# A decoder of two layers on one core: context loaded transposed, row vectors in two transfers, new priorities

## The chip, the cores and the metric

The kernel runs on one core of one Trainium2 chip. The metric is the device time of one execution in microseconds (us), lower is better. The core has five engines that matter here: PE (TensorE, matrix products; its weight loads are listed apart as PEld), DVE (VectorE), ACT (ScalarE), POOL (GpSimd), and SP (SyncE), which only issues transfers (DMA). Each engine works off its own queue in order, and semaphores order the engines among each other.

## The reference

Sixteen entries of 256 tokens with 256 features pass through two decoder layers in float32. Each of six sub-blocks is followed by a residual sum and a layer norm (`LN`, without weights):

```
x = LN(x + attn0(x))          # layer norm, q, k, v; ELU+1 feature maps; a 16 x 16 mix over the heads of each token;
                              # output product; then an MLP of width 1024 with GELU
x = LN(x + xattn0(x, ctx))    # 16 heads, keys and values from the context, window of 64 tokens to each side
x = LN(x + ffn0(x))           # six attention nodes of 8 heads, each fed by earlier nodes
x = LN(x + attn1(x))          # linear attention, causal cumulative sum
x = LN(x + xattn1(x, ctx))    # 16 heads, normed q and k, keys from the context, padding mask
x = LN(x + ffn1(x))           # product in the Fourier domain, plus a bias
```

`ctx` (16 x 256 x 256) enters twice: as keys and values of `xattn0`, and as keys and values of `xattn1`.

## The kernel before

Two partition blocks of 128 tokens (or features) and 256 columns make one slot of 128 x 512 float32; an entry has ten slots (`slot(s, n)`), and four entries are in flight (`NS = 4`, s = entry mod 4). An entry is loaded when the entry four before it is finished. A product needs its input with the features on the partitions. So nearly every product is preceded by a transposition on PE: `transposes` (line 704, matmuls against an identity at line 707) makes four 128 x 128 transposes into a PSUM bank, and an engine copies them out. For the context there are two such steps in each entry: `ctx_t` at the start (from slot RAW into slot CT, copied by ACT at line 1393) for the products `x_k` and `x_v` of the first cross attention, and `ctx_t2` late (a second load, named `again`, into slot AGAIN, and again copied into CT) for `y_k` and `y_v` of the second. CT is also the home of node 0 of the feed-forward in between, which is why the context is brought a second time.

`tokens` (line 711) and `features` (line 719) are the two forms of a 256 x 256 x 256 product: eight matmuls at lines 714 and 722. Attention scores are computed at lines 872 and 897, their maxima at 1233 (DVE), exponentials at 1466 (ACT), and the products with the values at 925. The mix of the first attention block runs on POOL (lines 1614 and 1624) with sums on DVE (1199, 1203).

The order of the work is not written out by hand. `entry_steps()` lists the 510 steps of an entry, each with its engine, an assumed duration, and the steps that it needs; `setup_steps()` does the same for the set-up, which folds weight matrices into each other. `program_plan()` then plays all 16 entries and the set-up through, and at each free engine takes the ready step of the earliest entry with the largest `tail`, the longest chain of durations that hangs on it. Each tail is multiplied with a random factor:

```
    rng = np.random.default_rng(720053)
    lean = [0.0 * v for v in rng.random(len(steps))]
    tail = [t * (1 + 0.3 * v) for t, v in zip(tail, rng.random(len(steps)))]
```

The result, `PLAN`, is the fixed queue of every engine. Weights of most products are streamed through a ring of four slots by SP, between the other transfers. The row vectors (13 biases and norm vectors, 256 long, copied to all partitions, tile `row`) come in one transfer of 1664 KB, which SP issues behind the operands of set-up node 2. They are needed first by DVE at line 1189, which adds the biases to q, k and v.

Of the kernel before, what the change touches and what calls it, by code (L numbers as in the profile page):

```python
# [11 lines left out]
ACT = mybir.ActivationFunctionType  # L12
AX = mybir.AxisListType.X

P = 128
# [53 lines left out]
ROWS = ["a_qb", "a_kb", "a_vb", "a_ob", "proj_b", "x_bo", "ln_g", "ln_b", "y_bq", "y_bk", "y_bo", "f_b", "n5_b"]  # L69
RSLOT = {n: i for i, n in enumerate(ROWS)}  # L70

SLOTS = 10
X, CT, XT = 0, 1, 2
RAW, AGAIN, Z = 6, 7, 7
# [20 lines left out]
SINGLE = range(4, BANKS)  # L95

# [49 lines left out]
def entry_steps():  # L146
# [13 lines left out]
    def layer_norm(n, ready, *also):  # L160
# [6 lines left out]
    ctx_t = through("ctx_t", 0, 0.44, "ACT", 0.49, load)  # L167
    z = layer_norm(1, load)
    z_t = through("z_t", 0, 0.44, "ACT", 0.9, z)
    raw = [through("a_qkv", a, 1.75, "DVE", 0.61, z_t, ("PE", "ctx_t", 0),  # L170
                   *((("PE", "a_qkv", a - 1),) if a else ()), also=(ctx_t,))
# [29 lines left out]
    x_k = through("x_k", 0, 1.75, "ACT", 1.8, ctx_t, ("PE", "z2_t", 0))  # L201
# [46 lines left out]
    for c in range(NODES):  # L248
# [11 lines left out]
        if c == NODES - 1:  # L260
            again = do("SP", "again", 0, 2.6, cv[c])
            ctx_t2 = through("ctx_t2", 0, 0.44, "ACT", 0.48, again, ck[c])
            y_k = through("y_k", 0, 1.75, "DVE", 0.66, ctx_t2, ("DVE", "centre", "y_k"))
            y_k = do("ACT", "y_k", 0, 0.48, y_k)
            y_k = do("DVE", "y_ks", 0, 0.6, y_k)
            y_k = do("ACT", "y_ks", 0, 0.5, y_k)
            y_k = do("DVE", "y_kn", 0, 0.65, y_k)
# [51 lines left out]
def program_plan():  # L319
# [14 lines left out]
    rng = np.random.default_rng(720053)  # L334
    lean = [0.0 * v for v in rng.random(len(steps))]
    tail = [t * (1 + 0.3 * v) for t, v in zip(tail, rng.random(len(steps)))]
# [59 lines left out]
    while events:  # L396
# [10 lines left out]
        for e in waiting:  # L407
            blocked = set()
            for i, t, n in sorted(waiting[e], key=lambda w: (
                    ((2.5 if e == "SP" else 1.5) if w[0] < 0 else w[0]) + (0 if kept_mode(w[2]) else 0.5) + lean[w[2]], w[1], w[2])):  # L410
# [64 lines left out]
def build(nc, x, ctx_in, mask, w_all, w_setup, cols, rows, ew, act_w, out):  # L475
    ctx = ExitStack()
    with ctx:
# [53 lines left out]
        in_vec = signal("s_loaded_vectors", 16)  # L531
        in_rows = signal("s_loaded_rows", 16)
# [11 lines left out]
        signals = ([setup_pe, setup_vec, setup_act, setup_pool, in_vec, in_rows, in_fourier] + list(in_w.values()) + in_ring + in_node + evicted  # L544
# [120 lines left out]
        def tensor(e):  # L665
# [76 lines left out]
            for i, op, a, units in PLAN["PE"]:  # L742
# [52 lines left out]
                elif op == "ctx_t":  # L795
                    e.wait_ge(*when("ctx", i))
                    transposes(take("misc", "ctx_t", i), slot(s, RAW)).then_inc(*tell(pe[s], "ctx_t mm", i))
                elif op == "ctx_t2":
                    e.wait_ge(*when("ctx again", i))
# [994 lines left out]
```

## Time and profile before

| | |
|---|---|
| median of three runs | 3605.32 us (3601.53 to 3610.42) |
| span of the profiled execution, first to last instruction | 3599.7 us |
| median less span (what lies around it) | 5.6 us |
| mean granted clock of PE over the span | 0.974 of full speed |
| busy: PE, DVE, ACT, POOL | 3245.1, 2282.5, 1713.9, 1019.3 us |
| transfers | 122.88 MB, mean 34 GB/s |

The profile comes from one further execution, whose own time is known as its span. Busy time of matmuls is modelled, since they overlap: the duration of one is longer than the distance to the next.

### The profile page before, as it was taken

The page shows a single profiled execution, that of the slowest core. Times are in us where ns is not written, and L with a number is a line of the kernel's source. Part 1 is how long each engine was busy: PE and PEld are TensorE (multiplying, and loading weights), DVE is VectorE, ACT ScalarE, POOL GpSimd, SP SyncE. Part 2 cuts the span into 40 slices and gives each one's busy share as a digit, 9 for nine tenths or more (in the row PEclk, how much of TensorE's full clock was granted, in tenths as well). Part 3 has the DMA queues.
Part 4 walks back from the last instruction along what each step waited for, and adds up shares of the span by engine and source line. Part 5 has one row for each costly group of instructions (what it writes and reads, how often), then busy time and mean ns, then how long its engine had stood idle before and what let it go on. Part 6 is the DMA issues. An engine that isn't in the chain of part 4 may idle for free.

```text
span 3599.7 us, 77605 instructions
## 1 busy us (share of the span) xinstructions
PE 3245.1 (90%) x31500; PEld 2402.1 (67%) x31500; DVE 2282.5 (63%) x4093; ACT 1713.9 (48%) x3466; POOL 1019.3 (28%) x795
## 2 busy tenths in 40 slices
PE   7899989999989989999999999999999999998876
PEld 6777666666676667766666776666677666766654
DVE  6665757647766766667676666767667576465633
ACT  1245454544545454554545555454555545554532
POOL 7942305103242504214060421506042150000000
PEclk9899999999999999999999999999999999999987
DMA  6211010100011101011010101101010110000000
GB/s 213 71 45 39 22 42 16 31 31 22 23 51 31 36 13 49 25 35 35 17 45 16 48 25 31 36 19 45 16 48 25 31 35 15 31 16 13 13 7 4
DMA packets 123132, 122.88 MB, mean 34 GB/s; under 512 B 9760, under 2 KB 122656, under 8 KB 122656
## 3 DMA queue, kind: packets, MB, share of 16 engines
q1 hardware_dynamic: 122784, 117.91, 10.9%
q8 instruction: 258, 4.23, 0.5%
q14 instruction: 90, 0.74, 0.1%
HBM read 113.69 MB, written 4.19 MB: 33 GB/s over the span
## 4 chain that ended last, share of the span: by engine, by line
PE 61%; DVE 13%; POOL 9%; ACT 8%; issue 7%; DMA 1%; SPq 0%; DVEq 0%; POOLq 0%; ACTq 0%
PE banks L722 16%; PE banks L714 13%; PE banks L897 7%; PE banks L925 6%; PE banks L872 6%; DVE nmx L1233 5%; POOL work L1614 5%; ACT work L1466 4%; POOL work L1624 3%; PE banks L707 2%; PE banks L883 2%; PE banks L729 2%; PE banks L932 2%; PE banks L901 1%; PE banks L1004 1%
## 5 line engine op out<-in xcount | busy, mean ns | idle before, releaser
L722 PE MATMUL banks<-work,weights 128*128 128x256 f32 x3584 | 861.9, 388 | 40.5 <-DVE work L1256 22.1
L1233 DVE TENSOR_REDUCE nmx<-banks 128x4 f32<-128x1024 f32 (+1 forms) x640 | 720.9, 1165 | 251.5 <-PE banks L872 249.1
L722 PEld LDWEIGHTS banks<-work,weights 128*128 128x128 f32 x3584 | 671.3, 192 | 177.1 <-issue 55.2
L1466 ACT ACTIVATE work<-banks 128x1024 f32<-128x1024 f32 (+1 forms) x640 | 596.5, 980 | 268.7 <-PE banks L901 266.9
L714 PE MATMUL banks<-weights,work 128*128 128x256 f32 x2688 | 661.0, 392 | 44.0 <-ACT work L1466 16.6
L714 PEld LDWEIGHTS banks<-weights,work 128*128 128x128 f32 x2688 | 505.0, 195 | 147.3 <-issue 47.7
L1624 POOL TENSOR_TENSOR work<-work 128x512 f32<-128x512 f32 x256 | 405.5, 1609 | 212.3 <-DVE work L1203 115.7
L897 PE MATMUL banks<-work 32*128 32x256 f32 (+1 forms) x5120 | 396.2, 396 | 46.2 <-issue 15.6
L872 PE MATMUL banks<-work 32*128 32x256 f32 (+1 forms) x5120 | 355.0, 393 | 36.2 <-issue 11.0
L1250 DVE TENSOR_TENSOR added<-work 128x1024 f32<-128x1024 f32 x192 | 261.5, 1363 | 171.7 <-ACT work L1466 164.1
L925 PE MATMUL banks<-work 128*32 128x256 f32 (+3 forms) x5632 | 334.6, 359 | 23.7 <-ACT work L1466 23.6
L1614 POOL TENSOR_TENSOR work<-work 128x512 f32<-128x512 f32 x256 | 341.0, 1358 | 49.8 <-DVE work L1199 32.2
L1658 POOL TENSOR_TENSOR work<-work,row 128x512 f32<-128x512 f32 x64 | 88.8, 1387 | 882.1 <-PE banks L707 882.1
L897 PEld LDWEIGHTS banks<-work 32*128 32x128 f32 x5120 | 213.3, 189 | 165.8 <-issue 97.3
L872 PEld LDWEIGHTS banks<-work 32*128 32x128 f32 x5120 | 234.9, 187 | 128.9 <-issue 108.3
L1365 ACT ACTIVATE work<-banks,cb 128x256 f32<-128x256 f32 x384 | 161.4, 473 | 251.7 <-PE banks L722 251.6
L925 PEld LDWEIGHTS banks<-work 128*32 128x32 f32 x5632 | 156.6, 110 | 163.8 <-issue 102.4
L1203 DVE TENSOR_REDUCE work<-work 128x32 f32<-128x512 f32 x256 | 173.1, 679 | 90.8 <-POOL work L1624 90.6
L1199 DVE TENSOR_REDUCE work<-work 128x32 f32<-128x512 f32 x256 | 172.2, 680 | 75.2 <-POOL work L1614 75.0
L1450 ACT ACTIVATE work<-banks 128x256 f32<-128x256 f32 x320 | 118.7, 385 | 189.7 <-PE banks L883 189.1
L707 PE MATMUL banks<-ident,work 128*128 128x128 f32 x896 | 140.1, 286 | 68.8 <-DVE work L1181 28.3
L901 PE MATMUL banks<-work,ones_bf 3*128 3x256 bf16 (+1 forms) x2560 | 191.4, 272 | 0.0
(157 smaller groups left out, 3518.3 us busy)
## 6 DMA issues: line engine op xcount, KB each, us to landing
weights<-in_w_all SPq DMA_DIRECT2D x322, 256.0 KB, 2.7
work<-in_w_setup SPq DMA_DIRECT2D x41, 256.0 KB, 5.5
work<-in_ctx SPq DMA_DIRECT2D x32, 256.0 KB, 2.9
work<-in_x SPq DMA_DIRECT2D x16, 256.0 KB, 3.0
out<-work SPq DMA_DIRECT2D x16, 256.0 KB, 2.2
weights<-in_w_all SPq DMA_DIRECT2D x1, 3072.0 KB, 16.9
row<-in_rows SPq DMA_DIRECT2D x1, 1664.0 KB, 10.1
mrow<-in_mask SPq DMA_DIRECT2D x16, 32.0 KB, 3.1
```

The costliest lines, as they stand in the source:

```text
L707: ins = e.transpose(b[:, f * 256 + c * P:f * 256 + c * P + P], src[:, c, f * P:f * P + P], ident[:, :])
L714: ins = e.matmul(b[:, m * 256:m * 256 + 256], xin[:, k, m * P:m * P + P], wslot(w)[:, k, :], start=(k == 0 and (m == 0 or closed)) if star ...
L722: ins = e.matmul(b[:, m * 256:m * 256 + 256], wslot(w)[:, k, m * P:m * P + P], xin[:, k, :], start=(k == 0 and (m == 0 or closed)) if star ...
L872: ins = e.matmul(b[g // 2][:, g % 2, cc * 256:cc * 256 + kk.stop - kk.start], q[32 * g:32 * g + 32, f, cc * P:cc * P + P], k[32 * g:32 * g ...
L897: e.matmul(b[g // 2][:, g % 2, o], k[32 * g:32 * g + 32, f, kc * P:kc * P + P], q[32 * g:32 * g + 32, f, qq], start=(kind != "x"), stop=False,
L901: ins = e.matmul(b[g // 2][:, g % 2, o], ones_bf[32 * g:32 * g + 3, :], upper(stored_nmax(s, a))[32 * g:32 * g + 3, qq], start=False, stop ...
L925: ins = e.matmul(b[32 * g:32 * g + 32, lo:hi], left, right[:, kc * 256 + lo - qq.start:kc * 256 + hi - qq.start], start=(kc == 0), stop=(k ...
L1233: e.tensor_reduce(nmax(s, n)[:, 2 * p:2 * p + 2, :], b, AX, ALU.max, negate=True).then_inc(*freed("max", n, p, i))
L1250: e.tensor_tensor(added[:, half], pt(half, 0, 4)[:, :, 0:S], pt(half, 0, 4)[:, :, S:2 * S], ALU.add).then_inc(*tell(vec[s], "added", a, i))
L1466: e.activation(dst, src, ACT.Exp).then_inc(*freed("exp", n, p, i))
L1614: e.tensor_tensor(big1, q.unsqueeze(2).broadcast_to([P, PH, NH, DH]), k.unsqueeze(1).broadcast_to([P, PH, NH, DH]), ALU.mult).then_inc(*te ...
L1624: e.tensor_tensor(big2, mix.unsqueeze(2).broadcast_to([P, PH, DH, NH]), v.unsqueeze(1).broadcast_to([P, PH, DH, NH]), ALU.mult).then_inc(* ...
```

## The change

1. The host hands `ctx` over with tokens and features exchanged. Each load goes straight into CT, and the steps `ctx_t` and `ctx_t2`, their PE transposes and their ACT copies are gone. The products `x_k`, `x_v` and `y_k` wait for the transfer itself. The second load may be issued once `ck` of node 5 has read CT; before, it waited for `cv` of node 5. The bytes and the form of the transfer stay the same.
2. The row vectors come in two transfers: the first three rows (biases of q, k and v) behind the first entry's `x`, the other ten behind the second entry's `x`; the one transfer behind node 2's operands is gone.
3. The tails are multiplied by five random factors in a row, one of up to 1.3 and four of up to 1.08, from other seeds. With the steps that are gone, this gives every engine another order.

```diff
@@ -164,11 +166,10 @@
     kept = do("DVE", "kept", 0, 0.9, load)
-    ctx_t = through("ctx_t", 0, 0.44, "ACT", 0.49, load)
     z = layer_norm(1, load)
     z_t = through("z_t", 0, 0.44, "ACT", 0.9, z)
-    raw = [through("a_qkv", a, 1.75, "DVE", 0.61, z_t, ("PE", "ctx_t", 0),
-                   *((("PE", "a_qkv", a - 1),) if a else ()), also=(ctx_t,))
+    raw = [through("a_qkv", a, 1.75, "DVE", 0.61, z_t,
+                   *((("PE", "a_qkv", a - 1),) if a else ()))
            for a in range(3)]
@@ -198,7 +199,7 @@
     x_t = through("x_t", 0, 0.44, "ACT", 0.48, x)
-    x_k = through("x_k", 0, 1.75, "ACT", 1.8, ctx_t, ("PE", "z2_t", 0))
+    x_k = through("x_k", 0, 1.75, "ACT", 1.8, ("PE", "z2_t", 0))
     x_v = through("x_v", 0, 1.75, "ACT", 0.56, clear)
@@ -258,10 +259,9 @@
         if c == NODES - 1:
-            again = do("SP", "again", 0, 2.6, cv[c])
-            ctx_t2 = through("ctx_t2", 0, 0.44, "ACT", 0.48, again, ck[c])
-            y_k = through("y_k", 0, 1.75, "DVE", 0.66, ctx_t2, ("DVE", "centre", "y_k"))
-            y_k = do("ACT", "y_k", 0, 0.48, y_k)
+            again = do("SP", "again", 0, 2.6, ("PE", "ck", c))
+            y_k = through("y_k", 0, 1.75, "DVE", 0.66, again, ("DVE", "centre", "y_k"), also=(("PE", "co", c - 1),))
+            y_k = do("ACT", "y_k", 0, 0.48, y_k, ("PE", "cv", c))
             y_k = do("DVE", "y_ks", 0, 0.6, y_k)
@@ -331,9 +331,9 @@
 
-    rng = np.random.default_rng(720053)
-    lean = [0.0 * v for v in rng.random(len(steps))]
-    tail = [t * (1 + 0.3 * v) for t, v in zip(tail, rng.random(len(steps)))]
+    for n, seed in enumerate(SEEDS):
+        spread = 0.08 if n else 0.3
+        tail = [t * (1 + spread * v) for t, v in zip(tail, np.random.default_rng(seed).random(len(steps)))]
     first, last = place["SP", "load", 0], place["DVE", "ln_n", 9]
@@ -407,7 +407,7 @@
             for i, t, n in sorted(waiting[e], key=lambda w: (
-                    ((2.5 if e == "SP" else 1.5) if w[0] < 0 else w[0]) + (0 if kept_mode(w[2]) else 0.5) + lean[w[2]], w[1], w[2])):
+                    ((2.5 if e == "SP" else 1.5) if w[0] < 0 else w[0]) + (0 if kept_mode(w[2]) else 0.5), w[1], w[2])):
                 if not idle[e]:
@@ -792,12 +793,6 @@
                     product(take("misc", "four", a), FOURIER[a][1]).then_inc(*tell(setup_pe, "four mm", a))
-                elif op == "ctx_t":
-                    e.wait_ge(*when("ctx", i))
-                    transposes(take("misc", "ctx_t", i), slot(s, RAW)).then_inc(*tell(pe[s], "ctx_t mm", i))
-                elif op == "ctx_t2":
-                    e.wait_ge(*when("ctx again", i))
-                    transposes(take("misc", "ctx_t2", i), slot(s, AGAIN)).then_inc(*tell(pe[s], "ctx_t2 mm", i))
                 elif op == "z_t":
@@ -837,11 +832,12 @@
                 elif op == "x_k":
-                    e.wait_ge(*when("ctx_t", i))
+                    e.wait_ge(*when("ctx", i))
                     arrived("x_k")
...
                     e.wait_ge(*when("cleared", i))
+                    e.wait_ge(*when("ctx", i))
                     arrived("x_v")
@@ -1028,7 +1024,7 @@
                 elif op == "y_k":
-                    e.wait_ge(*when("ctx_t2", i))
+                    e.wait_ge(*when("ctx again", i))
                     once("centred", "y_k", NH)
@@ -1183,9 +1179,7 @@
                     e.wait_ge(*when("a_qkv mm", a, i))
-                    once("rows")
-                    if a == 0:
-                        e.wait_ge(*when("ctx_t mm", i))
+                    once("first rows")
                     e.tensor_tensor(slot(s, A_QKV[a]), halves(at("a_qkv", a, i)), r_(("a_qb", "a_kb", "a_vb")[a]),
@@ -1385,12 +1379,9 @@
                         *freed("four", a))
-                elif op in ("ctx_t", "ctx_t2", "o_t", "x_t", "r_t", "y_t", "f_t"):
-                    dst = CT if op[:3] == "ctx" else XT
+                elif op in ("o_t", "x_t", "r_t", "y_t", "f_t"):
                     e.wait_ge(*when(f"{op} mm", i))
-                    if op == "ctx_t2":
-                        e.wait_ge(*when("ck mm", 5, i))
-                    e.activation(flat(s, dst), at(op, i)[:, :], ACT.Copy).then_inc(*freed(op, i))
+                    e.activation(flat(s, XT), at(op, i)[:, :], ACT.Copy).then_inc(*freed(op, i))
                 elif op == "c_t":
@@ -1702,9 +1693,6 @@
                         operand(f"{n}{a}", in_node[a], "node operands", a)
-                    if a == 2:
-                        e.dma_start(row[:, :, :].rearrange("p r n -> p (r n)"), rows.partition_broadcast(P)).then_inc(
-                            *tell(in_rows, "rows"))
                 elif op == "fourier":
@@ -1719,12 +1707,18 @@
                     e.dma_start(slot(s, X), of_entry(x, i)).then_inc(*tell(in_x[s], "x", i))
-                    e.dma_start(slot(s, RAW), of_entry(ctx_in, i)).then_inc(*tell(in_ctx[s], "ctx", i))
+                    if i == 0:
+                        e.dma_start(row[:, 0:FIRST_ROWS, :].rearrange("p r n -> p (r n)"),
+                                    rows[0:FIRST_ROWS * D].partition_broadcast(P)).then_inc(*tell(in_first_rows, "first rows"))
+                    elif i == 1:
+                        e.dma_start(row[:, FIRST_ROWS:, :].rearrange("p r n -> p (r n)"),
+                                    rows[FIRST_ROWS * D:].partition_broadcast(P)).then_inc(*tell(in_rows, "rows"))
+                    e.dma_start(slot(s, CT), of_entry(ctx_in, i)).then_inc(*tell(in_ctx[s], "ctx", i))
                     e.dma_start(small[s]["mrow8"][:, :], mask[i:i + 1, :].broadcast_to([P, S])).then_inc(
...
                 elif op == "again":
-                    e.wait_ge(*when("cv mm", 5, i))
-                    e.dma_start(slot(s, AGAIN), of_entry(ctx_in, i)).then_inc(*tell(in_ctx[s], "ctx again", i))
+                    e.wait_ge(*when("ck mm", 5, i))
+                    e.dma_start(slot(s, CT), of_entry(ctx_in, i)).then_inc(*tell(in_ctx[s], "ctx again", i))
                 elif op == "store":
@@ -1776,7 +1770,7 @@
     arrays = {
-        "x": a["x"], "ctx": a["ctx_1024"], "mask": a["mask_BxS2_bk0"],
+        "x": a["x"], "ctx": a["ctx_1024"].transpose(0, 2, 1), "mask": a["mask_BxS2_bk0"],
         "w_all": np.concatenate([w[n] for n in W_LOADED]), "w_setup": np.stack([w[n] for n in W_SETUP]),
```

Left out are the constants (`FIRST_ROWS = 3`, `SEEDS = (66172, 467317, 360552, 577980, 753377)`, slots RAW and AGAIN gone), the new semaphore for the first rows, and one wait of the `y_k` squares on ACT, which is now on `cv` of node 5 instead of the transposes.

## Rows read from the trace of the kernel before

**Rows 1.** The page: span, busy table, and two lines of its 40 slices.

```profile
span 3599.7 us, 77605 instructions
...
PE 3245.1 (90%) x31500; PEld 2402.1 (67%) x31500; DVE 2282.5 (63%) x4093; ACT 1713.9 (48%) x3466; POOL 1019.3 (28%) x795
...
PE   7899989999989989999999999999999999998876
...
PEclk9899999999999999999999999999999999999987
```

**Rows 2.** Windows: us, then busy us of PE, PEld, DVE, ACT, POOL; clock, DMA share, GB/s.

```profile
518.50:728.00 209.50, 190.00 (x1938) 136.69 (x1937) 142.58 (x248) 104.75 (x209) 59.94 (x44) 0.96 0.08 24
728.00:946.70 218.70, 198.07 (x1979) 143.51 (x1978) 140.48 (x247) 103.71 (x210) 57.91 (x45) 0.98 0.08 23
946.70:1145.80 199.10, 182.42 (x1781) 136.16 (x1783) 136.10 (x249) 100.10 (x205) 63.68 (x49) 0.97 0.12 36
1145.80:1363.50 217.70, 198.44 (x1985) 145.21 (x1978) 141.77 (x255) 107.50 (x220) 61.83 (x47) 1.00 0.10 30
...
1574.60:1785.40 210.80, 195.18 (x1946) 144.18 (x1945) 140.52 (x253) 106.39 (x216) 63.84 (x47) 0.99 0.11 31
3469.50:3599.70 130.20, 83.53 (x720) 58.29 (x712) 51.45 (x100) 41.48 (x85) 4.51 (x6) 0.79 0.02 5
```

**Rows 3.** Waits of PE's matmuls, window 1574.6 to 1785.4: releaser, total, times, longest.

```profile
PE banks L722 <- DVE work L1256: 2.0, 1, 2.0
PE banks L925 <- ACT work L1466: 1.7, 2, 1.2
```

**Rows 4.** Groups by line: busy, mean ns of one, idle before.

```profile
L707 PE MATMUL banks<-ident,work 128*128 128x128 f32 x896 | 140.1, 286 | 68.8 <-DVE work L1181 28.3 <-DVE ykb L1089 10.2 <-ACT work L1466 7.4
...
L1393 ACT ACTIVATE work<-banks 128x512 f32<-128x512 f32 x112 | 66.1, 597 | 80.8 <-PE banks L707 80.6
```

**Rows 5.** Timeline near 1865: start, us, engine, line.

```profile
1864.88 0.37 SPq L1727 DMA_DIRECT2D work<-in_ctx  x1
...
1867.80 1.09 PE L707 MATMUL banks<-ident,work 128*128 128x128 f32 x8
...
1868.73 3.62 PE L714 MATMUL banks<-weights,work 128*128 128x256 f32 x16
```

**Rows 6.** Timeline near 373: start, us, engine, line.

```profile
373.25 0.63 PE L707 MATMUL banks<-ident,work 128*128 128x128 f32 x4
...
374.65 1.97 PE L714 MATMUL banks<-weights,work 128*128 128x256 f32 x8 [0.78 <-ACT work L1393]
```

**Rows 7.** Who waited for the copies of line 1393 (us, times).

```profile
  PEld banks L714: 6.6, 8
  PE banks L714: 4.4, 6
```

**Rows 8.** Timeline of the first 26 us.

```profile
11.40 1.28 ACT L1393 ACT_TABLE_LOAD   x1 [11.40 <-PE banks L707]
...
13.31 1.28 ACT L1349 ACT_TABLE_LOAD   x1
...
18.18 3.78 PE L714 MATMUL banks<-weights,work 128*128 128x256 f32 x8 [1.11 <-ACT work L1365]
...
23.84 0.69 DVE L1189 TENSOR_TENSOR work<-banks,row 128x512 f32<-128x512 f32 x1 [4.52 <-issue]
...
25.38 1.49 POOL L1605 TENSOR_SCALAR work<-work 128x512 f32<-128x512 f32 x1 [17.90 <-ACT work L1416]
```

**Rows 9.** Windows of the start, to 135.7.

```profile
0.00:78.00 78.00, 54.79 (x263) 47.18 (x264) 47.77 (x107) 13.85 (x25) 51.07 (x63) 0.93 0.77 246
78.00:135.70 57.70, 52.48 (x244) 45.04 (x243) 34.42 (x59) 12.67 (x24) 56.69 (x43) 0.91 0.23 74
```

**Rows 10.** Transfers of the start: the page's row of in_rows, and below.

```profile
row<-in_rows SPq DMA_DIRECT2D x1, 1664.0 KB, 10.1
```

**Rows 11.** Timeline near 40.8: PE behind a transfer of set-up weights.

```profile
40.76 5.28 PE L757 MATMUL banks<-col,work 128*128 128x1 f32 x24 [3.83 <-DMA work<-in_w_setup]
```

More of the change, by code:

```diff
@@ L69 @@
 ROWS = ["a_qb", "a_kb", "a_vb", "a_ob", "proj_b", "x_bo", "ln_g", "ln_b", "y_bq", "y_bk", "y_bo", "f_b", "n5_b"]
+FIRST_ROWS = 3
 RSLOT = {n: i for i, n in enumerate(ROWS)}
@@ L73 @@
 X, CT, XT = 0, 1, 2
-RAW, AGAIN, Z = 6, 7, 7
+Z = 7
 A_QKV, ELU, MIX, BIG1, BIG2 = (3, 4, 5), (6, 7), 6, (7, 8), (9, 2)
@@ L95 @@
 SINGLE = range(4, BANKS)
+SEEDS = (66172, 467317, 360552, 577980, 753377)
 def quad(n):
@@ L531, in build @@
         in_vec = signal("s_loaded_vectors", 16)
+        in_first_rows = signal("s_loaded_first_rows", 16)
         in_rows = signal("s_loaded_rows", 16)
@@ L543, in build @@
         stored = [signal(f"s_stored{s}", 16) for s in range(NS)]
-        signals = ([setup_pe, setup_vec, setup_act, setup_pool, in_vec, in_rows, in_fourier] + list(in_w.values()) + in_ring + in_node + evicted
+        signals = ([setup_pe, setup_vec, setup_act, setup_pool, in_vec, in_first_rows, in_rows, in_fourier] + list(in_w.values()) + in_ring + in_node + evicted
                    + pe + vec + act + pool + in_x + in_ctx + in_mask + stored)
@@ L1530, in scalar @@
                     e.wait_ge(*when(f"{op} raw", i))
-                    e.wait_ge(*(when("ctx_t2 mm", i) if op == "y_k" else when("y_k_t mm", i)))
+                    e.wait_ge(*(when("cv mm", 5, i) if op == "y_k" else when("y_k_t mm", i)))
                     e.activation(flat(s, Y_K_SQ if op == "y_k" else Y_Q_SQ), flat(s, Y_K if op == "y_k" else Y_Q), ACT.Square).then_inc(
```

## The prediction

> **What bounds the kernel now.** I read the page first. PE is busy 3245.1 of 3599.7 us; the next engine, DVE, has 2282.5 [rows 1]. The slices show PE at nine tenths or more from the second slice almost to the end, with a granted clock of full speed (2.4 GHz) nearly all the way; the exceptions are the first slices and the last two, 0.8 and 0.7 [rows 1]. So the middle is PE's, but not by its work alone. I then cut the trace at the SP issues that load the next entry, which come once per entry [rows 2]. The reader should see that the kernel falls into a cycle: the four windows from 518.5 differ (209.5, 218.7, 199.1, 217.7 us), and the seven windows between loads from 1363.5 to 2838.6 all take 210.1 to 211.2 us, one of which is shown. In that one PE works 195.18 of 210.8 us and idles 15.6. In the four before, idle is 19.5, 20.6, 16.7 and 19.3 us, 19.0 on average. From 518.5 to the last load at 2838.6 lie 11 such windows, and PE is as full for about two more, so one microsecond per cycle is 13 us of the result. Last I read the waits inside the cycle: the largest is 2.0 us on a DVE norm, the next 1.7 us on exponentials [rows 3]; the idle time is many short waits in a fixed order, and the longest are not on a context transposition. The start is another regime: POOL is busy 56.69 of the 57.7 us from 78 to 135.7, and 51.07 of the first 78 [rows 9]; it only starts its attention work at 25.38 [rows 8]. The last 130.2 us have PE at work for 83.5 [rows 2].
>
> **Transposes that go.** Each entry loses `ctx_t` and `ctx_t2`, four 128x128 transposes each: 2 x 4 x 16 = 128 of the 896 matmuls of line 707 [rows 4]. In the steady cycle `ctx_t2` stands beside another group of four: eight begin at 1867.80 and the next product at 1868.73, so eight cost 0.93 us of PE's queue [rows 5]. That is the lower bound: 16 x 0.93 = 14.9 us. The upper bound is their share of busy time, 128/896 x 140.1 = 20.0 us [rows 4]. I take 17. The page "TensorE: Matmul & The Clock Gate" of the Trainium skill, Part 4, gives some 275 ns for such a transpose in a kernel's context and says that the mode does not count as PE being busy. The trace shows a duration near that (286 ns mean, [rows 4]) but a spacing of 116 ns, since they overlap [rows 5]. By the page's figure as a cost, 128 x 0.275 = 35 us would go instead of 17.
>
> **Copies that go.** 32 copies of 597 ns on ACT, 19.1 us [rows 4]. ACT is busy 106.4 of 210.8 us in a cycle [rows 2], so the copies lie beside other work except where PE stood behind one. All 112 copies of that kind held PE's products up for 6.6 us of weight loads and 4.4 of matmuls [rows 7], which are largely the same stops; one of `ctx_t2` shows it with 0.78 us [rows 6]. The share of 32 in 112 of 4.4 to 6.6 is 1.3 to 1.9 us. I take 1.5, bounds 0 and 6.6. What is late next at these places is the matmul's other inputs: after the change `y_k` stands directly behind the second context transfer. In the cycle that was issued at 1864.88 and the transposes started 2.92 us later [rows 5]. The SP issue now waits for `ck` of the last cell instead of `cv`, earlier by at most one product of 1.97 us [rows 6]. So I cost this wait at nothing; if its cover were gone, it would be at most 2.9 us per entry, 46 us. The streamed weights queue behind that SP wait and are released no later than before. The stronger waits in the new code (`x_v` on "ctx", `y_k` squares on `cv` of cell 5 instead of the transposes) name things that are finished tens of microseconds before or are read by earlier PE work; nothing.
>
> **Rows in two parts, and the start.** The first DVE addition ran at 23.84, after 4.52 us of idle time which the profile puts to no engine [rows 8]: the row vectors, whose transfer takes 10.1 us [rows 10], so issued at about 23.84 - 10.1 = 13.7. The products before it began at 18.18 and take 3.78, so the rows cost 23.84 - 21.97 = 1.9 us. Three of the 13 rows are 3/13 of 1664 KB, 384 KB, and are now issued right behind the first `x`; they will be there. Further, ACT loads a table for the context copy at 11.40, copies, and loads the exponential table at 13.31 for the first layer norm [rows 8]. Without the copy the second load can take the place of the first: 1.9 us more. So POOL may begin up to 3.8 us sooner, and POOL is what bounds to 135.7. Against it: the other 1280 KB now go before the node operands of the set-up, 5.2 us at the 246 GB/s of that window [rows 9], and PE already stands 3.83 us behind such operands at 40.76 [rows 11]. Before, the rows went behind the first six of these but ahead of the others, so only the first node's products are later. Bounds: 3.8 us gained, 5.2 lost. I take 1.5 gained. The DMA share later in the kernel is a tenth [rows 2] and covers everything else; the bytes and the shape of the context transfer are the same.
>
> **Priorities.** This is the part that no row prices directly. Every queue of every engine comes out of the planner, and the new factors together with the steps taken out give another order. What can change is idle time, 15.6 us per cycle, and the ends. The rows bound it thus: an order whose cycles idle like the four first ones, 19.0 us, loses 13 x 3.4 = 44 us; one that halves the idle time gains 13 x 7.8 = 101 us, which no window here shows. The waits are short and many, so an order can shave some of them, and there are two steps fewer in each entry that have to find a free PSUM bank. I lean a little to the gaining side: 0.6 us per cycle, 8 us. That is a choice; the range keeps both ends in part.
>
> **Sum.** 17 + 1.5 + 1.5 + 8 = 28 us. The profiled execution spans 3599.7 us; the median of the three runs is 3605.32, 5.6 us more for what lies around the span. Both fall alike: span about 3572, time 3605.3 - 28 = 3577 us. Without the order's 8 us it is 3585.
>
> **Rivals.** (A) *The new cycle idles more.* The transposes are gone, but the order locks into cycles with the 19.0 us of idle time of the first four windows. Then 44 us are lost and 20 gained: 3629 us, slower. It needs more than 1.5 us of extra idle time per cycle to eat the gain, and (20 + 10.8)/13 = 2.4 us to be measurably slower. For it: nearly all early windows are like that [rows 2], and the present cycle is among the least idle ones seen. Against it: its waits are spread, so nothing in particular must grow. (B) *The PE time freed turns into waiting.* If a chain of DVE maximum, ACT exponential and PE sets the cycle, removing work that filled a gap gives nothing: only the start and some of the transposes remain, 5 us, 3600 us, no change. For it: after PE's products the waits that end last are on DVE and ACT [rows 3]. Against it: in [rows 5] eight transposes lie in an unbroken run of PE work. (C) *A distinctly better order.* Idle time falls by 3 us per cycle to 12.6: 39 us in place of 8, so 3605 - 20 - 39 = 3546 us. (D) *Transposes cost their full duration.* Each is worth its 286 ns, not its spacing, 128 x 0.286 = 37 us in place of 17: 3557 us. [rows 5] speaks plainly against it. That is what the clock gate page's figure above would give.
>
> **How the numbers follow.** No change from a change can be told within about 0.3%, 10.8 us: 3594.5 to 3616.1. Chances: my forecast 0.42, its own range 3560 to 3594; (C) 0.24, 3520 to 3560; (D) 0.03; (B) 0.18; (A) 0.13, 3616 to 3640. That makes faster 0.69, same 0.18, slower 0.13. The range 3532 to 3612 leaves out the far end of (C), most of (A), together less than 2 in 10.
>
> **What the profile after would show.** 768 transposes on PE instead of 896, each cycle with 8 fewer PE matmuls, and PE's busy time per cycle down from 195.2 to about 194; if it falls by 2 us or more, (D) is right. The first DVE addition at about 20 instead of 23.84, and POOL's first work at 21 to 22. Windows between loads, once they repeat, of 209 us: 210.8 less 0.93, 0.1 and 0.6. Idle time per cycle near 15; 19 means (A), 16.5 (B), 12.6 (C). At `y_k`, no PE wait on the context transfer. I would be wrong if the cycle differs by more than 2 us either way, or if the end, where 46.7 of 130.2 us are idle [rows 2], grows or shrinks by more than 10: either is the order's doing and could outweigh all that I could price.

## The result, and the profile after

The changed kernel takes 3643.05 us (median of four runs, 3636.48 to 3646.29), the kernel before in the same comparison 3603.64. The ratio is 1.0114, 95% interval 1.0099 to 1.0129: 41 us slower. I had forecast 28 us faster, 3577 us, with 3532 to 3612 as the range. Of what I had listed, rival (A) comes nearest (3629 us, its own range 3616 to 3640, chance 0.13), and the time lies beyond that range too.

The page of the kernel after, its busy table and the granted clock in 40 slices (compare [rows 1]):

```profile
span 3641.2 us, 77305 instructions
...
PE 3257.8 (89%) x31372; PEld 2389.2 (66%) x31372; DVE 2277.5 (63%) x4093; ACT 1697.2 (47%) x3433; POOL 992.9 (27%) x795
...
PEclk9999999998999999999999999999999999999987
```

PE's busy time has risen by 12.7 us although it has 128 matmuls fewer, and its idle time (span less busy) has risen from 354.6 to 383.4 us. The slices hardly show it (both rows have one slice of eight tenths in the first third), but the mean granted clock has gone from 0.974 to 0.967.

Windows from load to load, columns as in [rows 2]:

```profile
511.60:726.40 214.80, 194.17 (x1988) 139.55 (x1981) 138.77 (x251) 103.41 (x209) 59.89 (x44) 0.95 0.08 22
...
1580.50:1794.40 213.90, 196.53 (x1938) 143.77 (x1937) 141.26 (x252) 105.45 (x215) 60.60 (x47) 0.98 0.10 31
1794.40:2009.40 215.00, 197.01 (x1938) 143.79 (x1937) 141.32 (x252) 105.61 (x215) 60.66 (x47) 0.98 0.10 31
...
2224.50:2440.60 216.10, 198.94 (x1938) 144.87 (x1937) 141.40 (x252) 105.72 (x215) 60.64 (x47) 0.97 0.10 31
...
3511.00:3641.20 130.20, 81.94 (x728) 56.85 (x720) 51.35 (x100) 41.84 (x84) 4.50 (x6) 0.79 0.02 5
```

The kernel again falls into a cycle, but of 213.9 to 216.1 us: 215.2 on average over the seven windows from 1364.4 to 2870.6, in place of 210.7. The count of PE matmuls is 1938, eight fewer, as it should be. Still PE's busy time is 196.5 to 199 us in place of 194.9 to 196.3 in the seven windows of before, at a mean granted clock of 0.97 to 0.98 in place of 0.98 to 0.99, and idle time is 17.2 to 18.3 us in place of 14.8 to 15.6. The end (130.2 us, PE busy 81.9) is as before. PE's longest waits in one of these cycles (releaser, total us, times, longest):

```profile
PE banks L928 <- DVE added L1244: 2.6, 2, 1.6
PE banks L723 <- ACT work L1387: 2.4, 1, 2.4
PE banks L868 <- DVE nmx L1227: 2.2, 2, 1.6
```

The second of them, 2.4 us, is the one that matters in e9 below. It is a product that stands behind a copy by ACT (`c_t`), not behind anything that the context touches.

The start, in the timeline (start, us, engine, line):

```profile
11.25 1.28 ACT L1343 ACT_TABLE_LOAD   x1 [11.25 <-DVE mv L1158]
...
16.28 3.75 PE L715 MATMUL banks<-weights,work 128*128 128x256 f32 x8 [1.20 <-ACT work L1359]
...
20.52 0.66 DVE L1183 TENSOR_TENSOR work<-banks,row 128x512 f32<-128x512 f32 x1
...
22.77 2.95 POOL L1596 TENSOR_SCALAR work<-work 128x512 f32<-128x512 f32 x2 [15.31 <-ACT work L1407]
```

There is one table load on ACT's way to the first layer norm, the first product starts at 16.28 instead of 18.18, the first DVE addition at 20.52 instead of 23.84, and POOL at 22.77 instead of 25.38 [rows 8]. The two transfers of the rows, size and us to landing:

```profile
row<-in_rows SPq DMA_DIRECT2D x1, 1280.0 KB, 9.5
...
row<-in_rows SPq DMA_DIRECT2D x1, 384.0 KB, 4.6
```

The instructions that move the context, their landing time, and who waited for them:

```profile
L1716 SPq DMA_DIRECT2D work<-in_ctx x16: 433/497/681, 3.6 to 2871.1; - x16
L1721 SPq DMA_DIRECT2D work<-in_ctx x16: 367/368/368, 354.1 to 3515.3; - x16
...
who waited for it (us, times):
busy tenths in 40 slices 0000000000000000000000000000000000000000
DMA to landing us min/median/max: 2.6/2.9/9.3
```

Nobody is listed: no engine waited for a context transfer, first or second.

### The profile page after: what moved, and what is told of

Same layout as the page of the kernel before. It is cut to its first block, busy times and chain, and to the rows that moved or that the text cites. A ratio compares the mean times of both kernels' runs of the same rounds, so it can differ in the third digit from the quotient of the medians.

```text
span 3641.2 us, 77305 instructions
## 1 busy us (share of the span) xinstructions
PE 3257.8 (89%) x31372; PEld 2389.2 (66%) x31372; DVE 2277.5 (63%) x4093; ACT 1697.2 (47%) x3433; POOL 992.9 (27%) x795
## 4 chain that ended last, share of the span: by engine, by line
PE 58%; DVE 20%; issue 8%; ACT 7%; POOL 6%; DMA 1%; SPq 0%; DVEq 0%; POOLq 0%; ACTq 0%
PE banks L723 17%; PE banks L715 12%; DVE nmx L1227 7%; PE banks L893 6%; PE banks L868 6%; PE banks L921 5%; POOL work L1615 3%; PE banks L831 3%; ACT work L1457 2%; POOL work L1605 2%; PE banks L730 2%; PE banks L928 2%; DVE work L1193 2%; DVE added L1244 1%; PE banks L879 1%
## 5 line engine op out<-in xcount | busy, mean ns | idle before, releaser
L723 PEld LDWEIGHTS banks<-work,weights 128*128 128x128 f32 x3584 | 678.8, 194 | 182.8 <-issue 50.1
L1615 POOL TENSOR_TENSOR work<-work 128x512 f32<-128x512 f32 x256 | 401.9, 1578 | 205.3 <-DVE work L1197 117.6
L893 PE MATMUL banks<-work 32*128 32x256 f32 (+1 forms) x5120 | 410.1, 407 | 46.5 <-DVE nmx L1227 17.9
L868 PE MATMUL banks<-work 32*128 32x256 f32 (+1 forms) x5120 | 365.4, 403 | 49.4 <-DVE nmx L1227 31.2
L1605 POOL TENSOR_TENSOR work<-work 128x512 f32<-128x512 f32 x256 | 327.5, 1293 | 77.1 <-DVE work L1193 61.0
L868 PEld LDWEIGHTS banks<-work 32*128 32x128 f32 x5120 | 243.6, 193 | 137.4 <-issue 114.2
L893 PEld LDWEIGHTS banks<-work 32*128 32x128 f32 x5120 | 216.5, 194 | 174.1 <-issue 78.4
L1250 DVE TENSOR_TENSOR work<-banks,work 128x256 f32<-128x256 f32 x192 | 80.3, 419 | 251.8 <-ACT work L1471 251.7
L879 PE MATMUL banks<-ident,nmx 128*128 128x128 f32 x640 | 131.5, 296 | 72.0 <-DVE nmx L1235 37.6
```

The source lines that it names most:

```text
L723: ins = e.matmul(b[:, m * 256:m * 256 + 256], wslot(w)[:, k, m * P:m * P + P], xin[:, k, :], start=(k == 0 and (m == 0 or closed)) if star ...
L868: ins = e.matmul(b[g // 2][:, g % 2, cc * 256:cc * 256 + kk.stop - kk.start], q[32 * g:32 * g + 32, f, cc * P:cc * P + P], k[32 * g:32 * g ...
L893: e.matmul(b[g // 2][:, g % 2, o], k[32 * g:32 * g + 32, f, kc * P:kc * P + P], q[32 * g:32 * g + 32, f, qq], start=(kind != "x"), stop=False,
L1605: e.tensor_tensor(big1, q.unsqueeze(2).broadcast_to([P, PH, NH, DH]), k.unsqueeze(1).broadcast_to([P, PH, NH, DH]), ALU.mult).then_inc(*te ...
L1615: e.tensor_tensor(big2, mix.unsqueeze(2).broadcast_to([P, PH, DH, NH]), v.unsqueeze(1).broadcast_to([P, PH, DH, NH]), ALU.mult).then_inc(* ...
```

## The experiments

For each kernel I also give the "planned end": the time at which `program_plan()` finishes its own play of the queues on its assumed durations. It is a number that the kernel's own planner computes, not a time of the chip; it is 3489 for before and 3507 for after.

**e1: the order kept.** The code of the kernel after, but the queues come from the steps and factors of the kernel before, with the context steps struck out. Shown is the line that strikes them; the rest of the edit puts the old steps and factors back into the planner.

```diff
+    plan = {e: [step for step in q if step[1] not in ("ctx_t", "ctx_t2")] for e, q in plan.items()}
     return plan, ring
```

> The code of the kernel after (context straight into CT, rows in two parts), but every engine's queue in the order of the kernel before, with only the ctx_t and ctx_t2 steps struck out. Theory 'order' (the loss comes from the new priorities, and the steps taken out are worth what I priced): 3604 - 20 = about 3585 us, range 3575 to 3592, cycle between loads about 209.6 us. Theory 'removal' (PE waiting for the second context transfer, or gaps left where the transposes stood, lose the time): 3625 us or more, cycle above 212. Theory 'freed time turns into waiting' (rival B): 3598 to 3604.

Measured: 3591.94 us, ratio 0.9974 (0.9965 to 0.9983), 9 us faster than before. The removal is a gain, so the theory "removal" is out, and the new order must cost the rest: 1.0114 - 0.9974 = 0.0140, 50 us (44 to 56, from the two intervals). But the gain, 9 us of the 20 that I had priced for transposes, copies and start, just reaches the range of theory "order" (3575 to 3592), and the cycle of 209.6 us that went with it did not come. The page of e1 and two of its windows:

```profile
span 3591.5 us, 77272 instructions
...
PE 3235.4 (90%) x31372; PEld 2393.4 (67%) x31372; DVE 2286.2 (64%) x4093; ACT 1695.9 (47%) x3433; POOL 1011.0 (28%) x795
```

```profile
1569.90:1781.30 211.40, 195.47 (x1938) 144.19 (x1937) 141.50 (x253) 105.44 (x214) 61.85 (x47) 0.98 0.10 31
1781.30:1992.60 211.30, 195.38 (x1938) 144.18 (x1937) 141.09 (x253) 105.57 (x214) 61.85 (x47) 0.98 0.10 31
```

The cycle has 8 matmuls fewer and takes 211.3 us; from the window at 1358.94 to the last load it averages 210.9, where before has 210.7. In the two profiled runs e1 is ahead by 0.9 us at the fifth load, by 2.3 over the eleven windows, and by 5.1 after the last load: most of the gain lies in the tail. Where did 0.93 us per cycle go? First the kernel before, behind the eight transposes of [rows 5] (timeline of PE), and the busy times of the same stretch (columns as in [rows 2]):

```profile
1872.28 1.15 PE L872 MATMUL banks<-work 32*128 32x256 f32 x16
1874.15 1.15 PE L872 MATMUL banks<-work 32*128 32x256 f32 x16 [0.72 <-issue]
1876.90 1.15 PE L897 MATMUL banks<-work 32*128 32x256 f32 x8 [1.60 <-issue]
...
1880.16 2.04 PE L722 MATMUL banks<-work,weights 128*128 128x256 f32 x8
1882.04 0.38 PE L883 MATMUL banks<-ident,nmx 128*128 128x128 f32 x2
```

```profile
1872.00:1880.00 8.00, 5.67 (x62) 3.80 (x61) 7.97 (x12) 1.29 (x2) 2.23 (x2) 0.81 0.08 27
```

DVE is busy 7.97 of 8.00 us here: this piece of the cycle is DVE's. The same piece in e1, with four transposes in place of eight:

```profile
1863.52 0.66 PE L711 MATMUL banks<-ident,work 128*128 128x128 f32 x4
1864.01 3.62 PE L718 MATMUL banks<-weights,work 128*128 128x256 f32 x16
1867.56 1.15 PE L871 MATMUL banks<-work 32*128 32x256 f32 x16
1869.88 1.15 PE L871 MATMUL banks<-work 32*128 32x256 f32 x16 [1.18 <-issue]
1872.63 1.23 PE L896 MATMUL banks<-work 32*128 32x256 f32 x8 [1.60 <-issue]
...
1875.99 3.48 PE L726 MATMUL banks<-work,weights 128*128 128x256 f32 x8
1879.31 0.38 PE L882 MATMUL banks<-ident,nmx 128*128 128x128 f32 x2
```

The products behind the transposes start 0.49 us after them instead of 0.93. Yet two rows further the score product waits 1.18 us instead of 0.72, so the half microsecond has become waiting: counted from the start of the transposes, that product begins after 6.35 us in before and 6.36 in e1. The profile puts this wait to no engine ("issue"); that it is for DVE is my reading, since DVE works almost without a break there in both kernels (in e1 7.96 of the 8.00 us from 1867.50). Then eight matmuls take from 1875.99 to 1879.31, 3.3 us, at a granted clock of 0.52, about the lower level (1.2 GHz), where before has 1880.16 to 1882.04, 1.9 us at 0.92. That is rival (B) at work in this place, for the transposes alone.

**e2 and e3: the factors exchanged.** e2 is the kernel after, each step with the factor it had before; e3 the kernel before with the new factors.

```diff
-    for n, seed in enumerate(SEEDS):
-        spread = 0.08 if n else 0.3
-        tail = [t * (1 + spread * v) for t, v in zip(tail, np.random.default_rng(seed).random(len(steps)))]
+    tail = [t * factor[step[:3]] for t, step in zip(tail, steps)]      # e2: factor of the same step in before
```

> The kernel after, but each step's tail is multiplied with the factor that the same step had in the kernel before; the planner makes a new order from them. Theory 'order': the order is not the old one, since the list of steps differs, so the time is that of a draw near the old one: 3575 to 3620. Theory 'removal': as the kernel after, 3635 to 3650.

> The kernel before with its context transposes, but with the five new factors on each step (1.33 on the steps of the context transposition, which have none). Theory 'order': if the new factors are poor as such, this is slower than before too, 3630 to 3665. Theory 'removal': it stays near before, 3590 to 3620. If factors mean little once the list of steps changes, any draw is possible and this one alone tells only how wide the draws lie.

Measured: e2 3691.86 us, ratio 1.0250 (1.0235 to 1.0265); e3 3683.82, 1.0226 (1.0209 to 1.0243). Both are slower than any range I had given them, and slower than both kernels. The old factors are 2.5% worse on the new list of steps than on their own, the new ones 1.1% worse on the old list than on theirs; and on either list the borrowed factors lose to the list's own (by 1.3% and 2.3%). So in these two trials a factor has no worth of its own; it picks one order for one list. Planned ends: 3544 and 3546.

**e4: the rows alone.** The kernel before with the two transfers of the rows, order kept (the edit is the diff's for `load`, `node` and line 1189).

> The kernel before with the row vectors in two transfers and nothing else changed, the order kept. My price: 1.9 us from the rows at most, and up to 5 us lost behind the larger transfer: 3599 to 3607. A theory that the earlier rows cost the start (set-up weights later) expects 3608 or more.

Measured: 3602.84 us, ratio 1.0004 (0.9992 to 1.0016): no change, and the interval holds a gain of up to 3 us and a loss of up to 6. But this run doesn't price the rows of the kernel after. Its start (timeline):

```profile
17.50 1.97 PE L709 MATMUL banks<-ident,work 128*128 128x128 f32 x8 [6.21 <-DMA work<-in_ctx]
...
24.40 0.69 DVE L1191 TENSOR_TENSOR work<-banks,row 128x512 f32<-128x512 f32 x1 [2.69 <-PE banks L716]
```

The 1280 KB of the second transfer now go ahead of the second entry's context. PE, which here still transposes that context, waits 6.21 us for it, its first product begins at 20.58 instead of 18.18, and the first addition comes at 24.40, later than before's 23.84, though its rows are there. In e1 and in the kernel after, which have no such transposes, it comes at 20.67 and 20.52.

**e5, e6, e7 and e11: other orders of the kernel after.** Only the list of seeds changes.

```diff
-SEEDS = (66172, 467317, 360552, 577980, 753377)
+SEEDS = (66172, 467317, 360552, 577980)    # e5
+SEEDS = (280, 10171, 20083, 30631)         # e6
+SEEDS = ()                                 # e7
+SEEDS = (1088, 100885, 300324, 400393)     # e11
```

> The kernel after with the first four of its five factors; the last, of up to 1.08, is left out. Nothing else changes. Theory 'order' (the time is set by which order the factors happen to give): it moves by more than 10 us in either direction; the planner's own end, on its assumed durations, is 3494 against 3507 for the kernel after and 3489 for before, and the four kernels so far lie 1.6 us on the chip apart for 1 us of the planner's, so 3623 us, range 3605 to 3635. Theory 'removal': 3635 to 3650, as the kernel after.

> The kernel after with another chain of four factors, the one whose planned end was lowest among some 20,000 tried for this list of steps: 3443 against 3507 for the kernel after. Theory 'order': 3542 us, range 3520 to 3580, so faster than before and after. Theory 'removal': no faster than before, 3600 or more. Theory 'the planner can't tell orders this near each other apart': 3590 to 3640.

> The kernel after with no factors at all; tails as the durations give them. Planned end 3514. Theory 'order': by the same relation 3650 us, range 3625 to 3680. If the five factors do harm as such and not through the order that they happen to give, this lies near before, 3580 to 3610.

> The kernel after with a third chain, found from another first factor; planned end 3453. Theory 'the planned end tells the order's worth': 3512 + 1.6 x 9 = 3527 us, range 3512 to 3550. If e6 was luck, 3580 or more.

**e10: a searched order of the kernel before.** The same search, with the context transposes and copies still in.

> The kernel before (with its context transposes and the rows in one transfer) under a chain of four factors, searched with the same effort as in e6: planned end 3456, against 3443 in e6 and 3489 for the kernel before. Theory 'order first': 3520 to 3560, well faster than before; and the rest of the change, taken out of e6, is worth the difference of the two, 10 to 20 us. If the order of e6 is only good because two steps are gone, this lies at 3590 or above.

Measured, beside each planned end:

| kernel | planned end | chip, us | ratio to before (95%) |
|---|---|---|---|
| e6, searched | 3443 | 3512.26 | 0.9746 (0.9731 to 0.9760) |
| e11, other chain | 3453 | 3530.55 | 0.9807 (0.9790 to 0.9824) |
| e10, searched, steps of before | 3456 | 3571.88 | 0.9917 (0.9902 to 0.9931) |
| before | 3489 | 3603.64 | 1 |
| e5, four factors | 3494 | 3644.03 | 1.0112 (1.0097 to 1.0127) |
| after | 3507 | 3643.05 | 1.0114 (1.0099 to 1.0129) |
| e7, no factors | 3514 | 3642.96 | 1.0110 (1.0078 to 1.0142) |
| e2 | 3544 | 3691.86 | 1.0250 (1.0235 to 1.0265) |
| e3 | 3546 | 3683.82 | 1.0226 (1.0209 to 1.0243) |

The same work with the same 31372 matmuls (after, e2, e5, e6, e7, e11) takes 3512 to 3692 us, depending on its order alone: 5%. That settles that the order is large enough to turn the sign. e7 and e11 came within the ranges of "order". e6 was faster than its range (3512; 3542 expected, 3520 to 3580). e5 missed (3623 expected, 3644 came: leaving out the fifth factor makes no difference to the time), and e10 missed, 12 us above its range and 60 us above e6 where I expected 10 to 20. The planned end thus sorts orders that it sees 50 us apart, but the gap between it and the chip runs from 69 us (e6) to 150 us (e5): before and e5, 5 us apart for the planner, are 40 us apart on the chip. The 18 us between the planned ends of before and after are too few to rely on. e6 is the fastest version I have, 2.5% faster than before and 3.6% faster than after. Its page and two cycles:

```profile
span 3506.4 us, 77283 instructions
...
PE 3205.2 (91%) x31372; PEld 2365.4 (67%) x31372; DVE 2288.1 (65%) x4093; ACT 1698.9 (48%) x3433; POOL 1003.2 (29%) x795
...
PEclk8999999999999999999999999999999999999997
```

```profile
1733.40:1939.60 206.20, 193.31 (x1937) 141.93 (x1937) 141.73 (x252) 105.54 (x214) 61.44 (x47) 1.00 0.11 32
1939.60:2146.00 206.40, 193.37 (x1938) 141.98 (x1937) 141.70 (x252) 105.53 (x214) 61.44 (x47) 1.00 0.11 32
```

Against the kernel after, with the very same 31372 matmuls: PE busy 52.6 us less (3205.2), idle 82.2 us less (301.2), a clock of 1.00 in every window between the fifth load and the last.

**e8: the context transposes made twice.** The kernel before, queues kept, 128 transposes more (shown for `ctx_t`; `ctx_t2` alike).

```diff
+                    b = take("misc", "ctx_t", i)
+                    transposes(b, slot(s, RAW))
-                    transposes(take("misc", "ctx_t", i), slot(s, RAW)).then_inc(*tell(pe[s], "ctx_t mm", i))
+                    transposes(b, slot(s, RAW)).then_inc(*tell(pe[s], "ctx_t mm", i))
```

> The kernel before, queues as they are, with the four transposes of each ctx_t and ctx_t2 made twice into the same bank: 128 more of them. Theory 'PE work counts at its spacing' (my term of 17 us): 15 to 20 us slower, 3617 to 3622. Theory 'freed time turns into waiting, and so added work fills waiting': 0 to 8 us slower. If both hold in part, the cost is like the 10 us that e1 gained.

Measured: 3613.13 us, ratio 1.0025 (1.0015 to 1.0036), 9 us slower. Adding 128 costs what removing 128 gains: 0.0025 x 3603 / 128 = 70 ns each (42 to 101 by the interval), between the two theories and below the spacing of 116 ns.

**e12: the same 128 transposes added to e6**, in front of each `x_k` and `y_k`.

```diff
-                    features(take("misc", "x_k", i), "x_k", slot(s, CT)).then_inc(*tell(pe[s], "x_k mm", i))
+                    b = take("misc", "x_k", i)
+                    transposes(b, slot(s, CT))
+                    features(b, "x_k", slot(s, CT)).then_inc(*tell(pe[s], "x_k mm", i))
```

> The kernel of e6 (the fastest so far, 3512 us), queues unchanged, with four transposes of the loaded context made on PE in front of each x_k and each y_k, into the bank that the product then overwrites: 128 matmuls more, no copy and no wait. In e6 the middle of the run shows full clock throughout, and PE idles 12.9 us of 206.2 in a cycle. Theory 'the price is the spacing where PE is full' : 128 x 0.116 = 15 us slower than e6, 3524 to 3530. Theory 'about 40 per cent of such work always falls into waiting', as in e1 and e8: 8 to 11 us, 3519 to 3524. Compared with before it is some 2.2 per cent faster either way.

Measured: 3517.94 us, ratio 0.9766 (0.9742 to 0.9791), 6 to 7 us slower than e6, just below both expected ranges. The two intervals overlap: from the ratios the difference is 7 us, with -3 to 17 open. So this run excludes neither theory, nor that they cost nothing here.

**e9: a wait filled.** The kernel after, queues kept, and 16 transposes of the identity on PE in front of `ck` of node 0, where PE waits for the copy of `c_t`. They add work that the result doesn't use.

```diff
+                    b = take("misc", "ck", a, i)
+                    if a == 0:
+                        for j in range(16):
+                            e.transpose(b[:, j % 4 * P:j % 4 * P + P], ident[:, :], ident[:, :])
                     e.wait_ge(*when("node", nk, i))
                     once("fold", "k", a)
-                    features(take("misc", "ck", a, i), f"ck{a}", slot(s, HOME[nk])).then_inc(*tell(pe[s], "ck mm", a, i))
+                    features(b, f"ck{a}", slot(s, HOME[nk])).then_inc(*tell(pe[s], "ck mm", a, i))
```

> The kernel after, queues unchanged, with 16 idle transposes of the identity on PE in front of the product ck of node 0, into the bank that this product overwrites. They need nothing and stand where PE waits 2.42 us in each cycle for the ACT copy of c_t. Theory 'the wait costs a second time through the clock' (after it the granted clock falls and 13 matmuls take 4.76 us in place of about 3): the fall goes, 1 to 1.7 us per cycle, so 10 to 22 us faster than the kernel after, 3621 to 3633. Theory 'the clock falls for other reasons' : no change, or up to 4 us slower, 3640 to 3647. If the filler comes late, up to 16 x 0.116 = 1.9 us per entry are lost, 3673 at worst.

First the place in the kernel after, on PE, and windows of 5 us around it:

```profile
1846.92 0.29 PE L897 MATMUL banks<-work,ones_bf 3*128 3x256 bf16 x4
1849.63 7.13 PE L723 MATMUL banks<-work,weights 128*128 128x256 f32 x24 [2.42 <-ACT work L1387]
```

```profile
1845.00:1850.00 5.00, 2.58 (x38) 1.62 (x31) 0.42 (x1) 4.94 (x11) 1.27 (x1) 1.00 0.17 52
1850.00:1855.00 5.00, 5.00 (x17) 4.11 (x16) 1.23 (x1) 2.24 (x4) 0.00 (x0) 0.66 0.01 2
```

After 2.42 us of waiting PE's products run at a mean granted clock of 0.66 in the window from 1850: the first 13 of the 24 matmuls take 4.76 us, 0.37 us each, and all 24 7.1 us. So it goes in nine of the ten windows from 938.7 on that have this wait (6.9 to 7.1 us). In the first of the ten it doesn't, after a wait as long:

```profile
995.28 5.42 PE L723 MATMUL banks<-work,weights 128*128 128x256 f32 x24 [2.50 <-ACT work L1387]
```

So such a wait often comes with the fall, not always. The same place in e9, and the clock of its products:

```profile
1863.31 0.29 PE L897 MATMUL banks<-work,ones_bf 3*128 3x256 bf16 x4
1863.53 1.97 PE L949 MATMUL banks<-ident 128*128 128x128 f32 x16
1866.03 5.45 PE L723 MATMUL banks<-work,weights 128*128 128x256 f32 x24 [0.53 <-ACT work L1391]
```

```profile
1866.03:1871.41 5.38, 5.38 (x25) 4.48 (x25) 1.23 (x1) 2.62 (x4) 0.00 (x0) 1.00 0.00 2
```

Now 24 matmuls take 5.45 us, 0.23 us each, at full speed, after a filler that leaves a wait of 0.53; and so in each of the nine windows from 1169.13 on. Two windows of e9 from load to load:

```profile
1596.40:1810.91 214.51, 199.12 (x1954) 145.13 (x1953) 141.45 (x252) 105.67 (x215) 60.64 (x47) 0.98 0.10 31
1810.91:2023.05 212.14, 195.40 (x1954) 143.29 (x1953) 141.30 (x252) 105.63 (x215) 60.60 (x47) 1.00 0.10 31
```

Two of the seven windows from 1384.25 on now show a clock of 1.00 and 212.1 us. In the other five the clock still falls some 170 us behind the load, as it also does in the kernel after (in the window of 1596.40 it is 0.58, 0.50 and 0.90 in three stretches of 5 us from 1766.40 on). Over the seven the mean is 213.6 us, in place of 215.2. So inside the cycle it is as the theory said, 1.6 us. But the whole kernel takes 3648.69 us, ratio 1.0129 (1.0114 to 1.0144), no faster than the kernel after: in the profiled run the fifth load comes at 521.23 instead of 511.64 us, the four windows behind it lose 10.2 us together, and the end 3.0. 6.7 of the 10.2 lie in the window from 950.63, where the filler stands behind the wait and not in it:

```profile
1006.79 3.68 PE L949 MATMUL banks<-ident 128*128 128x128 f32 x16 [2.43 <-ACT work L1391]
```

The expected 3621 to 3633 did not come. What this shows is one place where, in most cycles, an idle stretch is paid a second time through the clock; not what the clock costs the kernel as a whole.

## Why the prediction was wrong

**The step that failed** is the paragraph "Priorities": "I lean a little to the gaining side: 0.6 us per cycle, 8 us." In its place the new order costs 50 us (after against e1, 1.0114 against 0.9974). The forecast's 28 us were 8 for the order and 20 for the rest; what came, 41 us slower, is 50 lost and 9 gained. In the profiled runs the spans are 3641.2 and 3591.5, 49.7 apart with the same matmuls. By stretch: up to the fifth load the new order is 6 us ahead (511.6 against 517.6); over the eleven windows from there to the last load it loses 41.1 (2359.0 against 2317.9); in the rest it loses 14.6. By kind: 27.3 us more of PE's idle time (383.4 against 356.1) and 22.4 more of its busy time (3257.8 against 3235.4).

**Its bound was too narrow, and the reasons wrong.** I bounded the loss by idle time only, 13 x 3.4 = 44 us. The busy time I took as fixed, less the transposes. It isn't: the mean granted clock is 0.967, 0.972 and 0.982 in after, e1 and e6. With two levels, full and half speed, a mean clock c means 2(1 - c) of the span at the lower one: 240, 201 and 126 us. Half of the difference after less e1 is 20 us, near the 22.4 us of busy time; half of that of e1 less e6 is 37, against 30.2. The other orders agree: in the seven runs with 31372 matmuls (after, e1, e2, e5, e6, e7, e11) PE's busy time spreads over 70 us (3203 to 3273), and less half of the time at the lower level only over 22 (3122 to 3144). That is an account, not an experiment; e9 shows the mechanism at one place only. My reason for a gain, that many short waits can be shaved, says nothing of the draw. The fact that spoke the other way stood in my own text: the cycle of before was among the least idle ones to be seen. e2, e3, e5 and e7 show what that means: every order that the planner wrote afresh in these runs without a search takes 3643 to 3692 us. The five factors were no better than none (e7).

**The transposes: mechanism right, size off.** I took 17 us, bounds 14.9 and 20.0. With the copies, my 18.5 became 9.4 for all of e1, the earlier start included; e8 gives 9 for the same number added. The bounds were no bounds: I priced each transpose at its spacing in an unbroken run, and the run breaks some 5 us after them, where DVE is full. At the place read in e1 the time goes into waiting, as rival (B) said; that it does so elsewhere is not shown.

**The context's wait: right.** No engine waited for the context; I had costed it at nothing. The 1.5 us for the copies are not shown: no run takes out the copies alone, and e1's 9.4 us less e8's 9 leave no room to see them.

**Rows and start: the events nearly right, the worth open.** First addition at 20.52 (forecast about 20), POOL at 22.77 (21 to 22). I wrote that behind the larger transfer only the first node's products are later; e4 shows that the second entry's context is later too, and there it costs the whole gain of the start. e4 thus says nothing of the 1.5 us in the kernel after; e1 is 0.9 us ahead of before at the fifth load. A slip of reading besides, without weight for the sum: PE's slices in [rows 1] are not at nine tenths or more from the second on; the second and three more in the first half show eight.

**Rivals.** (A) had the right side and the mechanism in part, 3629 us; its sign, 19 us of idle time per cycle, did not come (17.2 to 18.3), since the rest of the loss is busy time. (C), a distinctly better order, exists, and far beyond what I gave it (e6, 3512 us), but it isn't the one this change took. (D) is out: e8 gives 70 ns per transpose, not 286. The 275 ns that the Trainium skill, "TensorE: Matmul & The Clock Gate", Part 4, gives (for bf16; these are float32) are likewise not the cost here.

**Open:** why e6 and e10, 13 us apart in planned end, are 60 us apart on the chip; why e9 is 9.6 us later at its fifth load; which waits make up the 50 us of the new order; and what sets off the second fall of the clock in the cycles of the kernel after.

## What to carry to other kernels

When a change alters the input of a planner that writes every queue, the new order can be the largest part of the change, as here, and must be measured apart: strike the steps out of the old order first (here 9 us gained), and only then let the planner write a new one (here 50 us lost, or 80 us gained after a search). Random priority factors belong to one list of steps (here they lost 1.1 and 2.5% on another); after an edit to the list, search them anew. With PE at 90% a removed matmul gained less here than its spacing in a dense run, some 70 ns in place of 116: look some microseconds ahead for the engine on which PE waits next. And a transfer moved to the front delays what then stands behind it (e4: 6.21 us of waiting for a context): read the whole start again, not only the wait that the move removes.

## What the runs showed of the hardware

A wait of PE can be paid twice: after one of 2.42 us, 24 products took 6.9 to 7.1 us in nine cycles of the kernel after, and 5.4 us in a tenth, after 2.50 us. Filling that wait with 16 float32 transposes went with 5.45 us in nine cycles of nine (e9), two of them with a window at 1.00 instead of 0.98. The Trainium skill, "TensorE: Matmul & The Clock Gate", Part 4, says that transposes do not count as PE being busy in the same way; this case's trace does not agree, here they were enough. And the same 31372 matmuls had 3203 to 3273 us of PE busy time, depending on the order (e11 and e2).
